# A nine-stage transformer tower on one core: gated norms with the root one tile behind, constant products at the ends of the plain norms, and the last block's marks spread by transfers and applied by VectorE

## The reference, cut to what matters

```python
def _layernorm(x, axis=-1, eps=1e-05):
    m = jnp.mean(x, axis=axis, keepdims=True)
    v = jnp.var(x, axis=axis, keepdims=True)
    return (x - m) / jnp.sqrt(v + eps)
...
h = h + L0_ffn(_layernorm(h))    # 8 experts, the best 2, hidden 128, gelu
h = h + L1_attn(_layernorm(h))   # 4 layers: norm, linear attention, norm, mlp
h = h + L1_ffn(_layernorm(h)); h = h + L2_attn(_layernorm(h)); h = h + L2_ffn(_layernorm(h))
h = h + L3_attn(_layernorm(h)); h = h + L3_ffn(_layernorm(h))

def L3_ffn(h):                    # "capacity" block, hidden 256
    logits = x @ gate_w + gate_b                      # 8 experts
    probs = jax.nn.softmax(logits, axis=-1)
    idx = jnp.argmax(probs, axis=-1)                  # one expert for each token
    kept = pos < C                                    # the first C tokens of each expert
    hmid = jax.nn.relu(jnp.einsum('ecd,edf->ecf', buf, w1) + b1[:, None, :])
    ybuf = jnp.einsum('ecf,efd->ecd', hmid, w2) + b2[:, None, :]
    y_tok = ybuf[idx, pos_g] * (prb * kept)[:, None]
    return jnp.nan_to_num(y, nan=0.0, posinf=10000.0, neginf=-10000.0)
```

## Time and profile before

| | |
|---|---|
| median of 3 runs | 3603.61 us (3602.79 to 3608.56) |
| the profiled execution | 3605.74 us |
| its span, first to last instruction | 3604.0 us |
| mean granted TensorE clock | 0.953 |
| busy: PE, PEld, DVE, ACT, POOL | 91%, 58%, 54%, 51%, 26% |

### The profile page before, as it was taken

One profiled execution on the slowest core, in us unless ns is written; L12 is line 12 of the kernel. 1 busy time (PEld: TensorE's weight loads), 2 busy tenths in 40 slices (PEclk: granted clock), 3 DMA queues, 4 the chain that ended last, 5 costly groups with the idle time before them and its releaser, 6 DMA issues. The chain is left out here.

```text
span 3604.0 us, 65545 instructions
## 1 busy us (share of the span) xinstructions
PE 3269.2 (91%) x24881; PEld 2107.3 (58%) x24881; DVE 1936.3 (54%) x4015; ACT 1833.1 (51%) x4202; POOL 944.7 (26%) x943
## 2 busy tenths in 40 slices
PE   6999989898989898988988979997699999989999
PEld 6999986544645555535756553333466666655444
DVE  4666645203545444435947844445699999952111
ACT  1333324466565656555653533334466666654665
POOL 0000001000100000102726712223477777740000
PEclk9999999899999999999989979999799999997999
DMA  2000000000000000000000013220000000000000
GB/s 71 15 15 14 12 16 3 11 1 7 3 4 4 4 3 4 3 4 7 2 8 1 1 35 69 56 56 16 17 5 5 5 4 5 4 22 3 7 9 9
DMA packets 41760, 48.59 MB, mean 13 GB/s; under 512 B 9142, under 2 KB 38936, under 8 KB 40984
## 3 DMA queue, kind: packets, MB, share of 16 engines
q1 hardware_dynamic: 41448, 44.39, 4.8%
HBM read 38.67 MB, written 2.38 MB: 11 GB/s over the span
## 5 line engine op out<-in xcount | busy, mean ns | idle before, releaser
L692 ACT ACTIVATE p_hidden<-p_hid_ps,net_bias 128x344 f32<-128x344 f32 x816 | 383.7, 548 | 251.6 <-PE p_hid_ps L648 177.6
L665 PE MATMUL p_y_ps<-p_hidden,net_down 128*64 128x344 f32 x1632 | 280.7, 466 | 0.0
L642 PE MATMUL p_hid_ps<-xn,net_up 64*128 64x344 f32 x1248 | 252.6, 485 | 8.2 <-PEq L312 4.6
L2350 POOL TENSOR_TENSOR p_qt<-p_qt,p_q_sum 97x512 f32<-97x512 f32 (+1 forms) x44 | 46.4, 1055 | 742.9 <-DVE p_q_sum L2304 742.9
L2655 DVE TENSOR_TENSOR p_hid<-p_silu,p_pair_ps 128x344 f32<-128x344 f32 x288 | 134.8, 508 | 173.7 <-PE p_pair_ps L2604 93.9
L2636 ACT ACTIVATE p_silu<-p_pair_ps 128x344 f32<-128x344 f32 x288 | 116.0, 454 | 202.5 <-PE p_pair_ps L2593 202.5
L1833 POOL TENSOR_TENSOR p_rot<-p_rot,p_cross 128x512 f32<-128x512 f32 x128 | 160.0, 1273 | 176.7 <-DVE p_cross L1970 176.7
L2771 PE MATMUL p_c_ps<-p_in,p_c1w 128*128 128x126 f32 (+5 forms) x960 | 173.0, 311 | 32.2 <-POOL p_in L2844 32.2
L1846 POOL TENSOR_TENSOR p_prob<-p_prob,p_total 128x1024 f32<-128x1024 f32 (+1 forms) x128 | 185.6, 1472 | 14.9 <-DVE p_total L1996 14.9
L665 PEld LDWEIGHTS p_y_ps<-p_hidden,net_down 128*64 128x64 f32 x1632 | 100.0, 136 | 151.5 <-ACT p_hidden L692 52.3
L642 PEld LDWEIGHTS p_hid_ps<-xn,net_up 64*128 64x128 f32 x1248 | 101.3, 188 | 127.6 <-ACT p_hidden L692 79.6
(11 more groups left out here) (441 smaller groups left out, 8042.4 us busy)
## 6 DMA issues: line engine op xcount, KB each, us to landing
p_row<-gated_rows SPq DMA_DIRECT2D x192, 86.0 KB, 2.9
p_x<-in_tok_x SPq DMA_DIRECT2D x32, 192.0 KB, 2.4
out<-h SPq DMA_DIRECT2D x12, 172.0 KB, 1.8
p_swapped<-xn SPq DMA_DIRECT2D x64, 32.0 KB, 1.9
p_c3w<-in_tok_c3w SPq DMA_DIRECT2D x1, 1280.0 KB, 9.4
thirds_fold<-in_L_fold SPq DMA_DIRECT2D x1, 1156.5 KB, 5.2
gated_w<-in_L2m_w SPq DMA_DIRECT2D x2, 512.0 KB, 4.1
p_val_high<-shared_values SPq DMA_DIRECT2D x1, 1024.0 KB, 6.8
```

What stands on the lines that cost most here:

```text
L642: mm = pe.matmul(hid_ps[k % ring][:, 0:TILE], w_up[half(g), n, :], x[half(g), cols(t)], start=True, stop=not experts)
L665: mm = pe.matmul(y_ps[u][half(g), 0:TILE], w_down[:, n, :], hid[k % hidden_ring][:], start=n == 0, stop=last and not experts)
L692: act.activation(hid[k % hidden_ring][:], hid_ps[k % ring][:, 0:TILE], func, bias=b_up[:, n:n + 1]).then_inc(act_done.sem, 1)
```

## The change

1. In `norm_phase`, after the last average, PE waits for tile 8 to be scaled and runs 12 products of constants into that tile's bank.
2. In `gated_norm_phase`, ACT's order becomes squares(s), root(s - 1). Where there is no centring (L2), two products of constants are added at every one of PE's 15 steps. In L3, the 16 products ahead of the first count go, and the last 12 become 14.
3. The marks of L3 stay 0 and 1 (`offset=0.0`, `marks16`). Its `mlp_phase` drops the 384 products of `banish`. SP writes the marks to DRAM (two transfers of 8 rows), waits, and reads back each row of each tile, broadcast to 128 partitions of bfloat16 (96 uses, two halves, 192 transfers, ring of 6). DVE multiplies each hidden tile by its row in place (384 instructions) before PE's downward products, and the tile's closing steps are spread over the masks of the next tile.

```diff
+                pe.wait_ge(scaled.sem, scaled.at(TILES - banks + 1))
+                for _ in range(12):
+                    pe.matmul(centered_ps[(TILES - banks) % banks][:], tower.ones[:], tower.banish[:, 0:4, :],
+                              start=True, stop=True)
...
+                    if not center:
+                        keep_busy(2)
                 for c in range(per_tile * TILES, CHUNKS):
                     judge(c)
                 if counting is not None:
-                    keep_busy(16)
                     count(0)
                     keep_busy(20)
                     count(1)
-                    keep_busy(12)
+                    keep_busy(14)
...
-                for s in range(TILES + 2):
+                for s in range(TILES + 1):
                     if s < TILES:
                         squares(s)
-                    if s >= 2:
-                        root(s - 2)
+                    if s >= 1:
+                        root(s - 1)
...
-                    for g in range(HALVES if experts else 0):
+                    for g in range(HALVES if experts and not by_rows else 0):
...
-                        pe.wait_ge(act_done.sem, act_done.at(k + 1))
+                        if by_rows:
+                            pe.wait_ge(masked.sem, masked.at(k + 1))
+                        else:
+                            pe.wait_ge(act_done.sem, act_done.at(k + 1))
...
+                if by_rows:
+                    for g in range(HALVES):
+                        sp.dma_start(outside[g, :, :], experts.marks16[D * g:D * g + EXPERTS, :]).then_inc(
+                            put_out.sem, 16)
+                    sp.wait_ge(put_out.sem, put_out.at(32))
+                for x in range(uses):
+                    t, e = x // EXPERTS, x % EXPERTS
+                    if x >= row_ring:
+                        sp.wait_ge(masked.sem, masked.at(HALVES * experts.parts * (x - row_ring + 1)))
+                    for g in range(HALVES):
+                        sp.dma_start(row[x % row_ring][:, g, :], outside[g, e:e + 1, cols(t)].to_broadcast(
+                            [P, TILE])).then_inc(landed[x % row_ring].sem, 16)
+                    if store is not None and e == EXPERTS - 1 and t >= 1:
+                        sp.wait_ge(y_read.sem, y_read.at(t))
+                        sp.dma_start(store[:, cols(t - 1)], finish.acc[:, cols(t - 1)]).then_inc(stored.sem, 16)
...
+                def mask(s):
+                    x = s // experts.parts
+                    for g in range(HALVES):
+                        k = HALVES * s + g
+                        dve.wait_ge(act_done.sem, act_done.at(k + 1))
+                        if g == 0:
+                            dve.wait_ge(landed[x % row_ring].sem, landed[x % row_ring].at(32 * (x // row_ring + 1)))
+                        dve.tensor_tensor(hid[k % hidden_ring][:], hid[k % hidden_ring][:], row[x % row_ring][:, g, :],
+                                          ALU.mult).then_inc(masked.sem, 1)
...
+                for t in range(TILES):
+                    for n in range(blocks if by_rows else 0):
+                        mask(blocks * t + n)
+                        if n == 4 and t >= 1 and in_parts:
+                            weigh(t - 1)
+                        if n == 6 and t >= 1 and in_parts:
+                            finish.compare(dve, t - 1)
+                        if n == (9 if in_parts else 4) and t >= 1:
+                            add(t - 1)
```

More of the change, by code:

```diff
@@ L594, in _ @@
                     pool.memset(restart[:, :, 0, 0:1], 0.0).then_inc(restarted.sem, 1)
[L595 removed]
+                for n in range(first_turn[1] if copy16 is not None and counting is None else 0):
                     at = columns_of(n)
                     pool.wait_ge(copied.sem, copied.at(n + 1))
[L598 removed]
+                    pool.tensor_scalar(copy16[:, at], rows_t[:, at], offset, None, ALU.add)
 def mlp_phase(tower, net, func, x, finish, load, experts=None, sum_into=None, store=None):
     nc, ring, span = tower.nc, 4, 2
[L604 removed]
+    hidden_ring, row_ring = 8, 6
     with phase(tower) as ph:
@@ L621, in mlp_phase @@
             load(ph)
+        by_rows = experts and experts.marks16 is not None
+        uses = TILES * EXPERTS if by_rows else 0
+        if by_rows:
+            row = [ph.sb(f"row{r}", [P, HALVES, TILE], BF16) for r in range(row_ring)]
+            landed = [ph.counts(32 * len(range(r, uses, row_ring))) for r in range(row_ring)]
+            put_out, masked = ph.counts(32), ph.counts(HALVES * steps)
+            outside = nc.dram_tensor(f"mark_rows{tower.phases}", [HALVES, EXPERTS, COLS], BF16, kind="Internal").ap()
         aux_sb = [ph.sb(f"aux_sb{u}", [P, TILE]) for u in range(2)] if finish.broadcast else None
@@ L642, in raise_hidden @@
                         mm = pe.matmul(hid_ps[k % ring][:, 0:TILE], w_up[half(g), n, :], x[half(g), cols(t)],
-                                       start=True, stop=not experts)
-                        if not experts:
+                                       start=True, stop=not experts or by_rows)
+                        if not experts or by_rows:
                             mm.then_inc(up_done.sem, 1)
-                    for g in range(HALVES if experts else 0):
+                    for g in range(HALVES if experts and not by_rows else 0):
                         k = HALVES * s + g
@@ L710, in _ @@
             def _(sp):
-                for t in range(TILES if store is not None else 0):
+                if by_rows:
+                    for g in range(HALVES):
[12 more added lines that the diff above has]
+                        sp.dma_start(store[:, cols(t - 1)], finish.acc[:, cols(t - 1)]).then_inc(stored.sem, 16)
+                for t in range(TILES - 1 if by_rows else 0, TILES if store is not None else 0):
                     sp.wait_ge(y_read.sem, y_read.at(t + 1))
@@ L733, with __init__ @@
 class Experts:
-    def __init__(self, marks, unmarked, parts):
-        self.marks, self.unmarked, self.parts = marks, unmarked, parts
+    def __init__(self, marks, parts, unmarked=None, marks16=None):
+        self.marks, self.parts, self.unmarked, self.marks16 = marks, parts, unmarked, marks16
     def of(self, n):
@@ L2425, in vector @@
         dve.wait_ge(self.compared.sem, self.compared.at(step))
+    def vector(self, dve, y, aux, cols, t):
+        u, step = t % 2, t + 1
+        tmp = self.tmp[u]
+        if not self.finite:
+            self.weigh(dve, y, aux, t)
+            return dve.tensor_tensor(self.acc[:, cols], self.acc[:, cols], tmp[:], ALU.add)
+        ends = self.ends[u]
         dve.tensor_tensor(ends[:, 0, :], ends[:, 0, :], ends[:, 1, :], ALU.add).then_inc(self.joined.sem, 1)
```

47 lines of the change are left out of this document (29 added, 18 removed).

## The result

The changed kernel takes 3517.0 us (median of 4 runs, 3514.2 to 3519.5) where the kernel before, run beside it, took 3605.0 (median of 4): ratio 0.975, 95% interval 0.9725 to 0.9775. The profiled execution took 3517.4 us with a span of 3515.6.

What follows compares the result with a forecast made beforehand. PE was taken as the bound (busy 91%), with much gated-norm work and the plain norms' followers at 1.2 GHz. Terms -16 - 13 - 19 + 8 - 14 = -54 gave about 3549 us against 3603.6, range 3522 to 3580.

Steps and rivals of the forecast that it cites:

- L2's norm: L2's gated norm, not centred: clock expected to stay low despite two products a step, +8 us; -6 if it rises.
- the plain norms and followers: 12 products lie in PE's stop at no price and raise the clock behind: 16 us saved, ends 0 and 28.
- L3's experts: Masks moved from PE to DVE: 19 us saved less 5 at the entry, net 14 saved.
- L0's norm: L0's centred gated norm: loop opens, 1.77 us a tile at held clock, tail 1.3 less: 13 us saved, lower end 8.
- L3's norm: L3's centred gated norm: spreads 13.2, tail 1.3, dropped 16 products 4.3: 19 us saved, ends 9 and 21.
- Rival (b): L2's gated norm: the clock rises, -6 in place of +8, total 3535 us; chance 0.28.
- I put PE's stops at 0.7 a tile: L3's experts: PE waits 0.7 us a tile as closing steps fall between masks; net 1.6 x 12 = 19 saved.
- The entry: Start of L3's experts: first downward product at about 8.7 us, then low clock: +5 us, ends 2 and 8.
- Some of the stretches will fall low anyway: Behind plain norms: gaps in the following stage keep some stretches at low clock, so 16 us saved of 20.
- (a): Clock falls in gated norms as before and plain norms' followers stay half slow: 3575 us; chance 0.17.
- (c): L3's experts gain nothing because DVE or late rows become the bound: -40, 3563 us; chance 0.12.
- (d): Slower than before, by a mask much dearer than 0.55 us, deciding above 0.78; at twice 0.52, 3665; chance 0.03.

Runs made afterwards that it cites:

- part 1 alone: The kernel before with only the 12 constant products behind the plain norms added: 3594.2 us against 3604.9, ratio 0.9968.
- the gated norms alone: The kernel before with only the three gated norms changed: 3553.3 us.
- the experts alone: The kernel before with only the last block's rows of marks by transfers and masks on VectorE: 3589.9 us, the stage -15.3.

## Why the prediction was off

The signs of three parts and the order of their sizes were right; one step had the wrong sign, and the sizes of the others lay on one side. Of the 34 us by which the two profiled executions differ more than forecast (88 and 54), L2's norm makes 12, the plain norms and followers 7, L3's experts 6, L0's norm 5 and L3's norm 4.

**L2's norm: the step that failed.** "So I expect it to stay low here too", +8, was wrong; it was -3.9. The step leaned on the 22.2 us at 93% busy and 0.50 of L0, and took from the rise behind constant products alone that two among the judging "do less than 16 in a row". The run without them shows what was read wrongly: even 21.00 busy of 21 us leaves the clock at 0.50 when the work is short float32 products with weight loads between, and with two dense ones a step it rose. A busy share in the record is not what the clock follows. The rise in L0 was misread besides: the 5.0 us before it were not constant products alone but 8 of them and then the products that turn the marks, by the trace of before:

```profile
674.17 3.57 PE L347 MATMUL p_spare_ps<-banish,ones 128*128 128x512 bf16 x8
677.53 2.27 PE L359 MATMUL p_spread_ps<-ident,p_wide 128*128 128x128 f32 x12
```

So the 16 in a row that the step asked for weren't needed there either. Rival (b), at 0.28, had it. The Trainium skill (TensorE: Matmul & The Clock Gate, What's actually happening) says that activity releases the throttle; the rise with the two products a step agrees with that, the 21.00 of 21 us at 0.50 doesn't if the recorded busy time is taken for activity. Of the -6 it forecast, 1.75 went to the first two tiles, still mostly at the low clock (2067.56 to 2072.05, 4.49 where two take 2.74 later).

**L3's experts: a size.** The step "I put PE's stops at 0.7 a tile" was mis-sized. PE alone was right: 22.9 predicted, 22.88 measured, from 25.21. The stops rested on masks 0.55 apart; they are 0.44 apart when they need not wait for each other, and the run that makes them wait costs 1.1 a tile. So 12 x 2.33 = 28.0 could be saved where 19 were booked; late rows took 1.9 of it (0.98 + 0.87 in two tiles) and the longer wait for ACT 0.36 in a third. The entry was right in place (first downward product 8.72 us after it, 8.7 predicted). What is left between 28.0 - 2.2 and the measured 20.0 is 5.8, the entry (+5 booked) and the last tile's masks. That rows come late at all, with a ring of six, wasn't seen. The 20.0 itself is one execution's: seven with the same masks and two transfers a row have the stage at 288.0 to 295.6 us, so 14.5 to 22 saved, and the slowest, with rows late for 35.1 us, is at the 14 that was forecast.

**Centred gated norms: two sizes.** The mechanism, PE as the bound and a clock that holds, was right in both norms (low for 6 us of L0's where it was 27, and for 11 of L3's where it was 42), and undoing the order of ACT takes both back. The tile was put at 2.90 - 1.13 = 1.77 and is 1.61. With that, L0's first spread to last average takes 20.5 us: 12.8 saved for 11.8. The other size is the tail. The 30 judging products were given 1.3 less; from their start to the end of the stage L0 is 20.9 - 16.6 = 4.3 us shorter, since at full clock the products take 3.6, and what stands behind them, taken as unchanged, is 1.7 shorter. In L3 spreads to last average saved 36.7 - 20.9 = 15.8 (13.2 booked, the entry included), the judging products 6.3 - 3.3 = 3.0 (1.3) and the dropped 16 products 4.2 (4.3); putting these back costs 3.4.

**Plain norms: a size, partly open.** These steps held: 12 products within the stop, the gap behind them at most 1.2 us, and the 7 us behind at 1.00 in all 15. That they have no price of their own held at the norms, but not for the whole: three stages further on give back 6.2 us, at the low clock for longer, in every run with 12, and the prediction had no such term. "Some of the stretches will fall low anyway", 16 of 20, didn't happen. In "all others" -23.4 was measured. But of this not all is part 1's: counted over the same stages, part 1 alone gives -16.4, and the gated norms alone, which change no code there, -5.7. That the first is the 16 that was booked is luck: it is 28.2 gained, the prediction's upper end, less 11.8 lost in five stages that are at the low clock for longer. The seven runs with 12 products and the new gated norms lie between -22.1 and -28.2, the two with 12 products and the old centred norms at -16.4 and -16.8. These two both have a linear attention and the norm behind it together 6.3 longer than the changed kernel has, by a low stretch within them. What links it to the gated norm far ahead of it, other than that the stages start at other times, stays open; the run with 18 products has it too, with the new norms.

**The parts help each other.** Alone they give 77 us, together 88. Two parts of it are seen: in the old gated norm of L0 the changed entry turned into a lower clock, +4.2, which the new one, low for 6 us of 38, doesn't suffer; and the experts alone saved 15 where the whole saved 20, with more of their rows late. Why more rows are late there isn't shown: an execution of nearly the same kernel, without L2's two products, has them late about as often (30 waits and 31), and saves 14.5, so this part may be scatter.

**The range.** Its low end, 3522, was rival (b) with a full part 1. It left out that the experts could save 28 and L3's norm 21, though both stood in the text as ends: ends of independent terms on the same side were not added up. The other rivals: (a) the clock fell in no gated norm for long; (c) PE hardly waits for DVE; (d) a mask costs less than assumed, not more. Two sums in the text were wrong and decided nothing. By its own formula a mask of 1.04 us makes the stage 384 x 1.04 + 47 - 305 = 141 us longer and the whole 101, so 3705 and not 3665. And a mask of 0.61 only fills the 22.9 us that PE needs for a tile; the formula's price for no gain is 0.67.

## What to carry to other kernels

When a stage is at half clock, look at which products TensorE runs and what they wait for, not only at how busy it is: one root taken a tile earlier, or two constant products a step, turned 51 to 70 us stages into 38 to 47. Before elementwise work moves from PE to DVE, count it from start to start and without waits between neighbours, since a needless wait cost 11 us here. And when single terms have ends on the same side, widen the range by more than one of them, and judge by stages where the whole scatters by 5 us.

## What was unexpected of the hardware

- PE recorded as busy for 21.00 of 21 us, at a granted clock of 0.50 throughout; with two 512-column bfloat16 products in each step of the same loop the clock rose within three tiles and stayed at 1.00 to the end of the judging.
- DVE products of a 128x344 float32 tile and a bfloat16 row last 0.52 us in the record and start 0.43 to 0.44 us apart; a wait for the one before makes it 0.55 to 0.57.
- Rows of marks broadcast to 128 partitions in two transfers of 688 bytes a partition kept the DMA engines busy 0.71 of the time and landed in 10.3 us; in one of 1376 bytes, the same total, 0.51 and 5.7 us.
- Behind a stop of PE of 1.6 to 2.5 us at the end of a norm the next 7 us had a mean clock of 0.76 or 0.77 in five cases of 14, behind one of 0.3 to 1.2 us it was 1.00 in all 15, and behind one of 2.8 to 3.8 us, before the change, 0.56 to 0.80 in all 15.
- The same 12 products that keep the clock up behind the norms are followed, in all nine executions with them, by more time at the low clock in the same later stages: 12.5 to 12.6 us and not 6.8 in one mlp, 23.9 and not 15.9 in one attention phase. Why isn't shown.
